# Attention and mixture of experts on one core: a quarter of the first row-maximum sets is moved from the prologue into the first turn

## What is computed

```
x = x + layernorm(attention(layernorm(x)))      # scores = (q.k + q.rel_k[clip(k-q)]) / sqrt(8), softmax over 512 keys
                                                # out = w @ v + sum_k w * rel_v[clip(k-q)]
x = x + layernorm(experts(layernorm(x)))        # shared MLP + the top-1 expert of 16, scaled by its sigmoid
```

## Time and profile before

| | us |
|---|---|
| median of three runs | 1610.67 |
| the profiled execution's own time | 1612.52 |
| its span, first to last instruction | 1610.8 |
| first score of turn 0 | 116.91 |
| turn 0, slots 0 to 63, from its first exponential | 76.2 |
| turn 0, slots 64 to 127 | 82.5 |

### The profile page before, as it was taken

The page is one execution under the profiler, slowest core; times in us unless marked ns, Lnnn a source line. Parts: engine busy times, 40 slices in busy tenths (PEclk is TensorE's granted clock), DMA queues, the critical chain, the costliest instruction groups (busy, mean ns, idle before and its releaser), DMA issues.

```text
span 1610.8 us, 67870 instructions
## 1 busy us (share of the span) xinstructions
PE 1509.4 (94%) x28642; PEld 1178.3 (73%) x28642; DVE 1228.3 (76%) x3580; ACT 1115.4 (69%) x2053; POOL 482.2 (30%) x678
## 2 busy tenths in 40 slices
PE   5789999998999999999999999999999999899993
PEld 2347777776778777877787777777878766568993
DVE  7996768787878887888788878887887335644997
ACT  4537767776777777777777777777776766236882
POOL 4532130223122312231223122312201101664576
PEclk9999999999999999999999999999999999999997
DMA  3468576765464456444544464445424562425561
GB/s 86 145 192 224 137 179 161 192 152 157 106 151 103 114 125 156 102 112 125 154 104 110 125 154 102 119 119 146 101 56 104 123 211 73 122 86 155 152 176 56
DMA packets 489136, 212.11 MB, mean 132 GB/s; under 512 B 330663, under 2 KB 462436, under 8 KB 488832
## 3 DMA queue, kind: packets, MB, share of 16 engines
q1 hardware_dynamic: 474112, 165.75, 42.2%
q0 software_dynamic: 14720, 42.03, 7.8%
HBM read 105.73 MB, written 102.85 MB: 129 GB/s over the span
## 4 chain that ended last, share of the span: by engine, by line
PE 64%; DVE 21%; SPq 5%; issue 4%; DMA 3%; ACT 2%; POOL 1%; ACTq 0%; DVEq 0%; POOLq 0%
PE pv L891 12%; DVE mx L1405 11%; PE mix L846 10%; PE sc L869 7%; PE rel L898 7%; PE sc L871 6%; PE mix L848 5%; PE sc L863 4%; PE sc L1054 2%; SPq L584 2%; PE rel L1000 1%; PE mix L908 1%; PE pv L1061 1%; PE mix L774 1%; PE sc L990 1%
## 5 line engine op out<-in xcount | busy, mean ns | idle before, releaser
L1146 ACT ACTIVATE w<-sc,escale 128x512 f32<-128x512 f32 x1024 | 685.9, 689 | 300.3 <-PE sc L871 176.2
L1405 DVE TENSOR_REDUCE mx<-mix 128x1 f32<-128x512 f32 x960 | 642.6, 683 | 187.3 <-PE mix L848 176.2
L846 PE MATMUL mix<-WE 128*32 128x512 f16 (+1 forms) x1968 | 388.8, 394 | 27.8 <-DVE mx L1405 16.4
L891 PE MATMUL pv<-w,shared_part 128*9 128x128 f32 x8192 | 373.1, 274 | 4.4 <-issue 4.4
L869 PEld LDWEIGHTS sc<-shared_part,Wt 96*128 96x128 f16 x5120 | 219.9, 97 | 81.5 <-issue 31.8
L848 PE MATMUL mix<-Wn,WE 128*32 128x350 f16 (+41 forms) x1968 | 275.7, 281 | 0.3 <-issue 0.3
L869 PE MATMUL sc<-shared_part,Wt 96*128 96x64 f16 x5120 | 258.1, 192 | 4.2 <-DVE mx L1405 1.9
L891 PEld LDWEIGHTS pv<-w,shared_part 128*9 128x9 f32 x8192 | 202.8, 90 | 75.2 <-issue 49.2
L898 PE MATMUL rel<-w,shared_part 128*32 128x128 f32 x5120 | 257.2, 273 | 0.0
L871 PE MATMUL sc<-shared_part 104*128 104x128 f16 x2560 | 247.6, 218 | 0.3 <-issue 0.3
L1131 ACT ACTIVATE WE<-qp,hmask 128x256 f16<-128x256 f16 x500 | 215.6, 499 | 21.2 <-PE sc L848 21.2
(11 more groups left out here) (266 smaller groups left out, 1967.0 us busy)
## 6 DMA issues: line engine op xcount, KB each, us to landing
qm_d<-ks POOLq DMA_DIRECT2D x48, 512.0 KB, 5.0
shared_part<-qm_d SPq DMA_DIRECT2D x32, 768.0 KB
kt_d<-ks SPq DMA_DIRECT2D x48, 256.0 KB
shared_part<-kt_d SPq DMA_DIRECT2D x128, 96.0 KB
xs_d<-zrow SPq DMA_DIRECT2D x5, 2056.0 KB, 11.5
vs_d<-vst SPq DMA_DIRECT2D x16, 576.0 KB
shared_part<-vs_d SPq DMA_DIRECT2D x32, 288.0 KB
orl_d<-rel_s SPq DMA_DIRECT2D x512, 8.0 KB
```

Of the source, the lines that this page charges most:

```text
L846: nc.tensor.matmul(nat[rows, :], lq[:, rows], kn[b2][:, at:at + S], start=True, stop=False, skip_group_check=True)
L891: mm = nc.tensor.matmul(pv[b2][32 * g:32 * g + 9, P * hh:P * hh + P], VC[j][:, b2, 0 if near else 1, h, :], wt[:, :, b2, h, :], start=(j = ...
L1146: nc.scalar.activation(weights, products, ACT.Exp, scale=escale[:, 0:1]).then_inc(s["exp_done"], 1)
L1405: nc.vector.tensor_reduce(mx[:, k:k + 1], nat[:], AX.X, ALU.max).then_inc(s["mx_done"], 1)
```

## The change

The loop ahead of the turns makes 96 of the 128 sets. The last 32, groups t = 2 and 3 of batch 1, which turn 0 needs from its slots 64 and 96 on, are made in turn 0. There the slots 0 to 63 make two sets and one set by turns, 96 in all: the 32 late ones in slots 0 to 20, then the 64 of the next turn's first batch, from slot 21 on. The lists of jobs on the two shared banks are made for each turn, as the first now has more. What depends on the sets moves along: their stores, the loads of `Qn`, ACT's by-head instructions of batch 2 (16 of them from ahead of the turns into slots 2 to 17, the others from slots 1 and 42 to slots 22 and 43), and four steps on ACT that write the keys of batch 3 (from slots 17 to 20 to slots 22 to 25). In SP's program `load_kv(0, 0)` stands right behind `load_rv`, ahead of the store of batch 2's queries and of the maxima of batch 1, group 0.

```diff
+    def sets_in(i, slot):
+
+        if i == 0 and slot < 2 * LATE_SETS:
+            return tuple(range(slot + (slot + 1) // 2 - LATE_SETS, slot + 1 + (slot + 2) // 2 - LATE_SETS))
+        return (slot,)
+
+    def slot_after(m):
+
+        return next(slot for slot in range(SLOTS) if m in sets_in(0, slot)) + 1
...
+    def jobs_of(i):
+        jobs = []
+            jobs += [("row max", m) for m in sets_in(i, slot)]
...
@@ SyncE, in turn @@
+                for t in (2, 3):
+                    if i == 0 and slot == slot_after(16 * t - 49):
+                        store_max(0, 1, t)
...
-                    if slot == 29:
+                    if slot == (35 if i == 0 else 29):
                         store_kv(i + 1, 1)
-                    if slot == 3:
+                    if slot == (slot_after(-1) if i == 0 else 3):
                         load_qn(i + 1, 0, 1)
-                    if slot in (35, 67):
+                    if slot in ((slot_after(31) if i == 0 else 35), 67):
                         load_qn(i + 1, 1, slot // 64)
-                    if slot % 16 == 1 and slot > 1:
+                    if i == 0:
+                        for m in range(15, 127, 16):
+                            if slot == slot_after(m):
+                                store_max(1, m // 64, m // 16 % NT)
+                    elif slot % 16 == 1 and slot > 1:
                         store_max(i + 1, (slot // 16 - 1) // NT, (slot // 16 - 1) % NT)
@@ SyncE, ahead of the turns @@
         load_rv()
+        sp.wait_ge(s["kc_zeroed"], NT)
+        load_kv(0, 0)
         store_qn(1, 0)
         store_max(0, 1, 0)
         sp.wait_ge(s["zeroed"], ZEROED)
-        sp.wait_ge(s["kc_zeroed"], NT)
         load_q(0, 0)
-        load_kv(0, 0)
         load_kv(0, 1)
         store_max(0, 1, 1)
         load_qn(1, 0, 0)
         store_q(1, 0)
-        store_max(0, 1, 2)
         store_kv(1, 0)
-        store_max(0, 1, 3)
         turns(sp, turn)
@@ TensorE, in turn @@
-                    wait_for_bank(pe, ("row max", slot), i, prev, nxt, nxt2)
-                    natural(i + 1, slot // 64, slot % 64, bank("row max", slot), abs(slot // 32 - slot // 8 % 4) > 1)
+                    for m in sets_in(i, slot):
+                        wait_for_bank(pe, ("row max", m), i, prev, nxt, nxt2)
+                        natural(i + 1 + m // 128, m // 64 % 2, m % 64, bank(i, "row max", m), abs(slot // 32 - slot // 8 % 4) > 1)
@@ TensorE, ahead of the turns @@
-        for k in range(128):
+        for k in range(128 - LATE_SETS):
...
-        pe.wait_ge(s["mx_done"], 128)
+        pe.wait_ge(s["mx_done"], 128 - LATE_SETS)
@@ ScalarE @@
+        first_prep_at = {10: 0, 15: 1, 16: 2, 22: 3, 23: 4, 24: 5, 25: 6}
...
+                    steps = first_prep_at if i == 0 and half == 0 else prep_at
+                    if (nxt2 if half else nxt) and slot - 64 * half in steps:
+                        step = steps[slot - 64 * half]
+                        prep(i + 1 + half, 1 - half, step, bank(i, "prepare", half, min(step, 2)))
...
+                    if i == 0 and earlier < 2 * LATE_SETS:
+                        for ahead, start, each in FIRST_BY_HEAD:
+                            pair = (earlier - start) * each
+                            if 0 <= pair < H:
+                                by_head(1, ahead // 2, ahead % 2, range(pair, pair + each))
+                        continue
...
-        by_head(1, 0, 0, range(H))
@@ VectorE @@
-                    row_max(i + 1, slot // 64, slot % 64, bank("row max", slot))
+                    for m in sets_in(i, slot):
+                        row_max(i + 1 + m // 128, m // 64 % 2, m % 64, bank(i, "row max", m))
...
+        for k in range(128 - LATE_SETS):
@@ constants @@
+LATE_SETS = 32
+FIRST_BY_HEAD = ((0, 2, 1), (1, 22, 1), (2, 43, 1))
```

More of the change, by code:

```diff
@@ L345, in slots_together, with bank @@
         return 4 if nxt and abs(slot // 32 - slot // 8 % 4) <= 1 else 2
-    shared = []
-    for slot in range(SLOTS):
-        shared.append(("row max", slot))
-        for half in range(2):
-            if slot - 64 * half in PREPARE_PE:
-                shared.append(("prepare", half, PREPARE_PE[slot - 64 * half]))
-        for half in range(2):
-            if slot - FINISH[half] in FINISH_PE[half]:
-                shared.append(("finish", half, FINISH_PE[half][slot - FINISH[half]]))
-    assert len(shared) % 2 == 0
-    place = {job: n for n, job in enumerate(shared)}
-    def bank(*job):
-        return mix[place[job] % 2]
+    def sets_in(i, slot):
[6 more added lines that the diff above has]
+        jobs = []
+        for slot in range(SLOTS):
+            jobs += [("row max", m) for m in sets_in(i, slot)]
+            for half in range(2):
+                if slot - 64 * half in PREPARE_PE:
+                    jobs.append(("prepare", half, PREPARE_PE[slot - 64 * half]))
+            for half in range(2):
+                if slot - FINISH[half] in FINISH_PE[half]:
+                    jobs.append(("finish", half, FINISH_PE[half][slot - FINISH[half]]))
+        assert len(jobs) % 2 == 0
+        return jobs
+    shared = [jobs_of(i) for i in range(NP)]
+    place = [{job: n for n, job in enumerate(jobs)} for jobs in shared]
+    def bank(i, *job):
+        return mix[place[i][job] % 2]
     def finishing(slot, i, prev):
@@ L369, in wait_for_bank @@
     def wait_for_bank(pe, job, i, prev, nxt, nxt2):
-        n, turns_back = place[job] - 2, 0
+        n, turns_back = place[i][job] - 2, 0
         while True:
             if n < 0:
-                if isinstance(i, int) and i == 0:
+                if i == 0:
                     return
-                n, turns_back = n + len(shared), 1
+                n, turns_back = n + len(shared[i - 1]), 1
                 nxt, nxt2 = True, nxt
-                prev = not isinstance(i, int) or i > 1
-            what, turn = shared[n], i - turns_back
+                prev = i > 1
+            what, turn = shared[i - turns_back][n], i - turns_back
             if what[0] == "row max" and nxt:
@@ L935, in turn @@
                         wait_for_bank(pe, job, i, prev, nxt, nxt2)
-                        prep(i + 1 + half, 1 - half, job[2], bank(*job))
+                        prep(i + 1 + half, 1 - half, job[2], bank(i, *job))
                 together = slots_together(slot, nxt)
@@ L948, in turn @@
                         wait_for_bank(pe, job, i, prev, nxt, nxt2)
-                        finish(i - half, half, job[2], bank(*job))
+                        finish(i - half, half, job[2], bank(i, *job))
         def prologue(n, b2, step, mix):
@@ L1176, in turn @@
                 for half in range(2):
-                    if (nxt2 if half else nxt) and slot - 64 * half in prep_at:
-                        step = prep_at[slot - 64 * half]
-                        prep(i + 1 + half, 1 - half, step, bank("prepare", half, min(step, 2)))
+                    steps = first_prep_at if i == 0 and half == 0 else prep_at
+                    if (nxt2 if half else nxt) and slot - 64 * half in steps:
+                        step = steps[slot - 64 * half]
+                        prep(i + 1 + half, 1 - half, step, bank(i, "prepare", half, min(step, 2)))
                 due = (slot,)
@@ L1193, in turn @@
                     if (prev or half == 0) and slot - FINISH[half] in finish_at[half]:
-                        finish(i - half, half, finish_at[half][slot - FINISH[half]], bank("finish", half, 1))
+                        finish(i - half, half, finish_at[half][slot - FINISH[half]], bank(i, "finish", half, 1))
         prep(0, 0, 1, mix[0])
@@ L1610, in turn @@
                 if nxt:
[L1611 removed]
+                    for m in sets_in(i, slot):
+                        row_max(i + 1 + m // 128, m // 64 % 2, m % 64, bank(i, "row max", m))
                 for half in range(2):
                     if (nxt2 if half else nxt) and slot - 64 * half in prep_at[half]:
[L1614 removed]
+                        prep(i + 1 + half, 1 - half, prep_at[half][slot - 64 * half], bank(i, "prepare", half, 3))
                 for n, half, since in finishing(slot, i, prev):
@@ L1620, in turn @@
                         step = steps[since]
-                        finish(n, half, step, bank("finish", half, 0 if step == 6 else 2))
+                        finish(n, half, step, bank(i, "finish", half, 0 if step == 6 else 2))
                     for at, part in place_at[half]:
                         if since == at:
-                            place_tokens(n, half, part, bank("finish", half, 3))
-        for k in range(128):
+                            place_tokens(n, half, part, bank(i, "finish", half, 3))
+        for k in range(128 - LATE_SETS):
             row_max(0, k // 64, k % 64, (*mix, *sc)[k % 4])
@@ L1647, in _ @@
             if since >= SLOTS - FINISH[0]:
-                place_tokens(last, 0, part, bank("finish", 0, 3))
+                place_tokens(last, 0, part, bank(last, "finish", 0, 3))
```

2 lines of the change are left out of this document (1 added, 1 removed).

## The result

The changed kernel takes 1620.5 us in the median of 6 runs (1618.64 to 1624.61) against 1612.24 for the kernel before (6 runs, 1607.13 to 1614.75): a ratio of 1.0057, 95% interval 1.0038 to 1.0076. 1611 was forecast, at most 1620. The profiled execution took 1619.81 us, 7.3 more than that of before.

What follows compares the result with a forecast made beforehand. DVE was taken to bound the prologue and PE the turns; -13.9 + 9.2 + 3.3 + 1.5 = +0.1 us gave 1610.8 on the median, stated as 1611, range 1602 to 1620 (the forecast's own 1607 to 1616, chance 0.42).

Steps and rivals of the forecast that it cites:

- Term 1: Gate of turn 0: first score moves from 116.91 to 103.0 (100 to 106), -13.9 us (-16.9 to -10.9).
- bit under 1 us for the semaphore: At the gate: time assumed between the end of the first query tile's transfer and PE having it.
- rival 1: Key tile slips between transfers, gate at 100, DVE's room swallows the sets: net -5.4, 1605.3 us; chance 0.28.
- rival 3: SP held up 5.1 us issuing the key tile, gate at 106: net +3.2, 1613.9 us; chance 0.10.
- Term 2: Slots 8 to 63 of turn 0: 28 more sets at PE's price of 0.33 us each, +9.2 us.
- Term 3: Slots 0 to 7 of turn 0: four more reductions plus 0.9 for the clock, +3.3 us (+1.3 to +5.8).
- DVE paces the crowded slots: Turn 0's bunches of six sets: PE falls to DVE's pace through the two banks, +7.1, 1617.8 us; chance 0.20.
- Term 4: Turn 0's crowded slots: PE and DVE coupled through two shared banks, PE only two sets ahead, +1.5 us (0 to +5).
- From slot 64 on turn 0 is as before: Second half of turn 0: no change, again 82.5 us, since all waits are on counters of the same work.

Runs made afterwards that it cites:

- kept_warm: The changed kernel with 36 unused matmuls of 512 columns in PE's wait for the query tile; ratio to the kernel before 1.0033.
- spread: The changed kernel with each second additional set of slots 0 to 63 placed between values matmuls; ratio to the kernel before 1.0006.
- half_reduce: The changed kernel with DVE reducing only 256 of 512 columns per set in turn 0's slots 0 to 63; slots 8 to 55 took 68.6 us against 75.0.
- zero_behind: The changed kernel with SP waiting for the second masked query's store before slot 92's store of zeros; ratio to the kernel before 1.0033.
- only_key_first: The kernel before with only the first key tile's load moved ahead, all 128 sets in the prologue; ratio to the kernel before 0.9992.

## Why the prediction was wrong, step by step

**Term 1, the gate: right.** -13.9 was said, against -13.3 at the first score (103.59 for 103.0) and -12.9 at the first exponential. The steps behind it hold: query load at 96.46 (95.6 was said), 7.1 us from its issue to the score (7.0), release by a DMA. The "bit under 1 us for the semaphore" is an estimate: in the kernel before the first load of x, 262 KB issued at 0.80, is through at 3.0 at the earliest by the bytes moved till then, and DVE, which waits for it, begins at 3.75. The tile did not slip in between (rival 1), and SP was not held up while it issued it (rival 3): it took 2.1 us for the five DMAs, 85.85 to 87.90. The 5.1 us of that rival and of the upper bound are what SP took for this tile in the kernel before, 95.12 to 100.22; why it took longer there was not shown. ACT's weight copies came at 89.33, 11 us sooner and not 6.5, which changed nothing. That the size fits within a microsecond is partly luck, as the nine traces of this order lie between 102.57 and 106.63, two of them above the bound of 106.

**Term 2, PE's price of a set: right.** With reductions of half the length, slots 8 to 55 cost 68.6 us where 0.33 us a set gives 68.2.

**Term 3, slots 0 to 7: right within 0.6.** +3.9 for +3.3. The clock was at 0.50 from 97.4 to 107.6 us, in the wait and in the first 3 us of the turn. No run shows the 0.9 that I took for it, nor the 1.8 of the rival "DVE paces the crowded slots": by `kept_warm` it was worth 1.2 to 1.5 us. What I had to go by was one stretch of the kernel before, where it was at 0.50 from 23.1 to 30.0 us around PE's idle time from 20.4 to 26.4, the last 3.6 us with PE at work.

**Term 4, coupling: the step that failed.** It said "PE needs ... 3.9 us; DVE needs 6 x 0.60 = 3.6 and begins 0.8 us later. They are level", and "on the whole DVE has room: ... a share of 0.80", and took +1.5 us, at most 5. Measured were 18.18 - 9.2 = 9.0. DVE's total was right, 70.0 us by the prediction and 71.84 measured. Two things were wrong for this stretch. The 0.60 is the step from one reduction to the next when both banks are full; a bank comes free only at the end of its reduction, 0.68 to 0.69 us after its start. And a share of busy time says nothing where an engine may run ahead by two only: what counts is the time from one use of a bank to the next, 1.29 us, against what PE has to do in it, two sets of 0.32 and one score, 0.22 (far) or 0.47 (near). In the kernel before, sets two places apart in slots 8 to 63 lie at least 1.57 us apart, more than the round trip. That this is also why turn 2 could run at 0.82 of DVE with PE full is likely (two near slots at 0.80 are 1.6 us) but was not shown. The rival "DVE paces the crowded slots" named the place, the two banks. Its price, 0.60 a set instead of 0.33, gave +7.1 and 1617.8; what it said against itself, that the values give DVE 3 us, is true but no help: in that time DVE had already emptied both banks and was idle (0.72 us before 195.10).

**"From slot 64 on turn 0 is as before": wrong as well, by 3.0 us.** "All waits there are on counters of the same work" is true, but the order in time between two queues is no counter. SP came to its zeros 3.2 us earlier in the half, and so they overtook POOL's store; why SP was earlier was not traced further. In two of eleven versions with the zeros ahead (`spread`, `kept_warm`) the half took only 82.8 and 83.1 us; the late stores were there too (kt store 46.8 and 47.3 us after slot 64, before 43.4), but what of it reached PE varied, and why is open.

Together: 7.5 too little in term 4 (9.0 for 1.5), 3.0 missing behind slot 64, 1.0 in term 1 and 0.6 in term 3 make the start of turn 1 come 12.1 us later where 0.1 was forecast. (The prediction's own range says that the bounds of terms 2 to 4 are halved; term 2 has none, and 1607 to 1616 comes out with those of terms 1, 3 and 4.)

## What to carry to other kernels

Where two engines hand over through a few buffers, don't weigh their shares of busy time: take the round trip of one buffer (fill, read, both semaphores) from a timeline and lay it beside what the first engine does between two uses of it. Before costing added work at its price, look at where it stands in the order, since moving the same sets behind or between other work gave back about a third of what these slots lost. And an engine that gets ahead can change what stands first on the DMA queues, as SP did here by 3.1 us: list the large transfers that nobody waits for, and see what small one they may now overtake.

## What the runs showed of the hardware

- A small store took very different times to be seen as landed, by what had been issued before it: that of the maxima 2.5 to 7.9 us, that of the masked queries 2.8 us to 8.8 and, in `half_reduce`, 10.1. What stands ahead may come from another engine: POOL waited 8.81 us for its store with SP's zeros ahead of it (the kernel after), and 2.84 with them behind it (`zero_behind`).
- A wait put where the engine's queue is idle anyway can shorten a stretch: with one wait more on SP, slots 64 to 127 took 81.1 us for 85.4.
- In `zero_behind` slots 32 to 39 took 14.6 us instead of 11.8. There DVE's small split of maxima takes 2.02 us for its usual 0.17, and ends when POOL's subtraction does (DVE's line, then POOL's):

```profile
156.85 2.02 DVE L1440 TENSOR_SCALAR ms<-mx 128x16 f16<-128x16 f32 x1
```
```profile
156.72 2.12 POOL L1924 TENSOR_TENSOR ks<-WE,ks 128x1024 f16<-128x1024 f32 x1
```

The kernel before has such a meeting (DVE 235.78 to 237.20, POOL 235.01 to 237.16), and so has `only_key_first` (DVE 108.23 to 109.46, POOL 107.30 to 109.43). In each of the three DVE's instruction ends 0.03 to 0.04 us after POOL's; the cause is shown by no run.
